# Attention in four chained layers: projection applied to the values, denominators inverted as four columns

## The reference

```python
qkv = einsum('bchw,oc->bohw', x, qkv_w)
qkv = depthwise_conv_3x3(qkv, dw_w)
q, k, v = split(qkv, 3); q, k = l2norm(q), l2norm(k)      # tokens are the 16384 pixels
attn = softmax(einsum('bnc,bmc->bnm', q, k) * temperature, axis=-1)
out = einsum('bnm,bmc->bnc', attn, v)
return einsum('bchw,oc->bohw', out, proj_w)               # 48x48
```

## Time and profile before

| | |
|---|---|
| median of 3 runs | 7465.26 us (7460.11 to 7467.92) |
| the profiled execution | 7462.4 us, its span 7460.1 us |
| attention stage, first score to last copy of the sums | 326.75 to 3114.90 us |
| TensorE busy in it | 2765.76 us |
| VectorE busy in it | 2643.70 us |
| ACT busy in it | 2368.25 us |

### The profile page before, as it was taken

The page is one execution under the profiler, slowest core; times in us unless marked ns, Lnnn a source line. Parts: engine busy times, 40 slices in busy tenths (PEclk is TensorE's granted clock), DMA queues, the critical chain, the costliest instruction groups (busy, mean ns, idle before and its releaser), DMA issues. The chain is left out here.

```text
span 7460.1 us, 169553 instructions
## 1 busy us (share of the span) xinstructions
PE 6090.7 (82%) x68803; PEld 2679.5 (36%) x69312; DVE 6843.6 (92%) x6229; ACT 5240.9 (70%) x5318; POOL 3429.0 (46%) x1801
## 2 busy tenths in 40 slices
PE   6899999999999999899767777777777777766330
PEld 3333333333333333366323333333333333333220
DVE  7799999999999999899789999999999999986776
ACT  3388888888888888633468888888888888842000
POOL 2000000000000000000169999999999999974777
PEclk9899999999999999999889999999999999987665
DMA  2200000000000000000110000000000000022333
GB/s 42 61 8 8 8 11 8 8 8 8 8 8 11 8 8 8 4 6 7 35 46 6 6 6 6 6 6 6 6 6 6 6 6 6 6 56 74 83 83 82
DMA packets 130880, 146.51 MB, mean 20 GB/s; under 512 B 52524, under 2 KB 111692, under 8 KB 129244
## 3 DMA queue, kind: packets, MB, share of 16 engines
q1 hardware_dynamic: 104160, 82.28, 4.0%
q0 software_dynamic: 24576, 50.36, 2.6%
q10 hardware_dynamic: 1440, 3.75, 0.3%
HBM read 98.55 MB, written 37.75 MB: 18 GB/s over the span
## 5 line engine op out<-in xcount | busy, mean ns | idle before, releaser
L1790 POOL TENSOR_TENSOR k_image<-k_image,s_b 128x1024 f32<-128x1024 f32 x1152 | 2700.8, 2355 | 118.1 <-ACT k_image L1703 83.5
L710 ACT ACTIVATE att_prob<-att_scores,a_bound,a_temp 128x1024 f32<-128x1024 f32 x2048 | 2357.0, 1202 | 420.8 <-PE att_scores L653 420.8
L721 DVE TENSOR_TENSOR att_prob_lo<-att_prob 128x1024 f16<-128x1024 f32 x2048 | 2429.0, 1238 | 139.4 <-ACT att_prob L710 123.0
L638 POOL TENSOR_TENSOR k_image<-k_image,att_rden 48x512 f32 x32 | 67.7, 2116 | 2990.4 <-DVE att_rden L733 2990.4
L1703 ACT COPY k_image<-h_du 128x1024 f32<-128x1024 f32 x1152 | 1166.4, 1013 | 322.9 <-PE h_du L1637 322.3
L1753 DVE TENSOR_TENSOR_SCAN h_state_odd<-h_keep,k_image 128x1024 f32<-128x1024 f32 x576 | 1378.4, 2509 | 0.0
L653 PE MATMUL att_scores<-att_queries,att_keys 32*128 32x512 f16 (+1 forms) x20480 | 1294.0, 377 | 21.5 <-DMA att_queries<-qk_halves 18.8
L1709 ACT ACTIVATE h_keep<-h_keep,h_decay 128x1024 f32<-128x1024 f32 x1152 | 1256.7, 1091 | 74.7 <-PE h_keep L1626 51.2
L670 PE MATMUL att_sums<-att_prob,a_values 128*64 128x512 bf16 x8192 | 1124.9, 395 | 0.0
L1626 PE MATMUL h_keep<-h_rows,h_spread 128*128 128x512 bf16 x2303 | 699.0, 385 | 510.6 <-DVE h_state_odd L1753 263.1
L653 PEld LDWEIGHTS att_scores<-att_queries,att_keys 32*128 32x128 f16 (+1 forms) x20480 | 439.7, 93 | 776.2 <-ACT att_prob L710 379.3
(11 more groups left out here) (295 smaller groups left out, 7021.1 us busy)
## 6 DMA issues: line engine op xcount, KB each, us to landing
y_rows<-h_y_sb SPq DMA_DIRECT2D x1024, 3.0 KB
att_queries<-qk_halves SPq DMA_DIRECT2D x124, 128.0 KB, 2.2
parts<-t_part SPq DMA_DIRECT2D x48, 192.0 KB, 2.5
h_rows<-parts SPq DMA_DIRECT2D x128, 72.0 KB
b_shared<-cells,b_index POOLq DMA_INDIRECT x512, 2.6
qk_halves<-qkv_hi SPq DMA_DIRECT2D x128, 48.0 KB, 1.6
cells<-b_shared SPq DMA_DIRECT2D x4, 1536.0 KB, 5.1
att_keys<-qk_halves SPq DMA_DIRECT2D x32, 128.0 KB, 2.7
```

The source lines that it names most:

```text
L710: nc.scalar.activation(prob[:, u % RING, :], scores[:, u % SLOTS_S, :], ACT.Exp, bias=bound[:, 0:1], scale=temp[:, 0:1]).then_inc(prob_rea ...
L721: nc.vector.tensor_tensor(prob_lo[:, u % RING, :], prob[:, u % RING, :], prob_hi[:, u % RING, :], ALU.subtract).then_inc(low_ready, 1)
L1790: nc.gpsimd.tensor_tensor(drive[k % 3], du_sb[k % 3], b[:, c * CH:(c + 1) * CH], ALU.mult).then_inc(drive_ready, 1)
```

## The change

The sum over keys and the projection are both linear, so the projection is moved from the sums to the values. In `turn`, the 8 transposes become 8 f32 matmuls that turn v and multiply it by `out_w`, now 48x48 (twice, for the two partition ranges). To keep the f16 halves of `values` in range, the first stage divides `out_w` by a bound of each output channel and keeps the bound in `out_scale`: one more absolute value on ACT, two small matmuls on TensorE, five operations on VectorE, in place of two copies there.

In the attention stage the projection matmul goes. ACT's copy at unit 6 now takes 113 rows. At unit 12 VectorE adds the two partial sums (`total`). SP stores the two denominator rows in DRAM (`den_rows`), loads them as 128 partitions x 2 x 4, VectorE adds and inverts them at unit 18 (`join_den`, `invert`: 128x4), SP stores that in DRAM and loads it back as 48 equal rows of 512, and from unit 28 VectorE makes 8 products of 48x64, three units apart (`divide`). SP's loop over blocks is unrolled; its query loads now have these five DMAs between them.

```diff
-PROJECT_AT = 12
-INVERT_FROM = 18
+TOTAL_AT = 12
+INVERT_AT = 18
+DIVIDE_FROM = 28
 ...
@@ load_and_prepare: tensor, vector
+            pe.wait_ge(out_absolute, 1)
+            nc.tensor.matmul(ps_o[:, 0:C], all_ones[:, :], out_abs[:, :], ...)
+            nc.tensor.matmul(ps_o[HI, C:C + 1], out_abs[:, :], all_ones[:, 0:1], ...)
-            for rows_in, one in ((slice(32, 64), V_ONE), (slice(96, P), 64 + V_ONE)):
-                then(nc.vector.tensor_copy(out_w[rows_in, LO], ident[rows_in, one:one + 1].broadcast_to([32, C])))
             count_quarter(3)
+            dve.wait_ge(out_summed, 2)
+            then(ts(out_inv[:, 0, :], ps_o[:, 0:C], 0.25, 1e-30, ALU.mult, ALU.max))
+            then(nc.vector.reciprocal(out_inv[:, 1, :], out_inv[:, 0, :]))
+            for part in (LO, HI):
+                then(tt(out_w[part, :], out_w[part, :], out_inv[part, 1, :], ALU.mult))
+            then(ts(out_scale[HI, :], ps_o[HI, C:C + 1], 0.25, 1e-30, ALU.mult, ALU.max))
@@ project_qkv: turn
-                        last = nc.tensor.transpose(turned[:, b, t, :], v_sb[part, t * P:(t + 1) * P], ident[part, part])
+                        last = nc.tensor.matmul(turned[:, b, t, :], v_sb[part, t * P:(t + 1) * P], out_w[part, :], start=True,
+                                                stop=True)
@@ attend: sync
+            def spread_den(b):
+                sp.wait_ge(sums_copied, b + 1)
+                for side in range(2):
+                    row = side * CHUNK + V_ONE
+                    sp.dma_start(den_rows[b, side:side + 1], sums_sb[row:row + 1, :]).then_inc(den_stored, 16)
+                sp.wait_ge(den_stored, 32 * (b + 1))
+                wait_past(sp, joined, b)
+                sp.dma_start(den[:, :, :], den_rows[b].rearrange("s (p k) -> p s k", p=P)).then_inc(den_loaded, 16)
+
+            def spread_inverse(b):
+                sp.wait_ge(inverted, b + 1)
+                sp.dma_start(inverse_rows[b].rearrange("(p k) -> p k", p=P), inverse[:, :]).then_inc(inverse_stored, 16)
+                sp.wait_ge(inverse_stored, 16 * (b + 1))
+                wait_past(sp, added, b)
+                sp.dma_start(rden[HI, :], inverse_rows[b].partition_broadcast(C)).then_inc(inverse_loaded, 16)
+            for n in range(2, NQB):
+                sp.wait_ge(scores_ready, (n - 1) * UNITS)
+                load_queries(n, n % 2)
+                spread_den(n - 2)
+                spread_inverse(n - 2)
@@ attend: tensor
-            def project(b):
-                pe.wait_ge(sums_copied, b + 1)
-                nc.tensor.matmul(sums[0:SPAN, b % 2, :], out_w[:, :], sums_sb[:, :], start=True, stop=True).then_inc(projected, 1)
@@ attend: scalar, copy_sums
-                nc.scalar.copy(sums_sb[:, :], sums[:, b % 2, :]).then_inc(sums_copied, 1)
+                wait_past(act, den_stored, 32 * b)
+                nc.scalar.copy(sums_sb[0:SPAN + 1, :], sums[0:SPAN + 1, b % 2, :]).then_inc(sums_copied, 1)
@@ attend: vector
-                nc.vector.reciprocal(rden[HI, q], sums[LO, b % 2, q]).then_inc(inverted, 1)
-                nc.vector.tensor_tensor(rden[HI, q], sums[HI, b % 2, q], rden[HI, q], ALU.mult).then_inc(divided, 1)
+            def total(b):
+                dve.wait_ge(sums_copied, b + 1)
+                nc.vector.tensor_tensor(sums_sb[HI, :], sums[HI, b % 2, :], sums_sb[LO, :], ALU.add).then_inc(totalled, 1)
+            def join_den(b):
+                dve.wait_ge(den_loaded, 16 * (b + 1))
+                nc.vector.tensor_tensor(inverse[:, :], den[:, 0, :], den[:, 1, :], ALU.add).then_inc(joined, 1)
+            def invert(b):
+                nc.vector.reciprocal(inverse[:, :], inverse[:, :]).then_inc(inverted, 1)
+            def divide(b, piece):
+                dve.wait_ge(totalled, b + 1)
+                dve.wait_ge(inverse_loaded, 16 * (b + 1))
+                nc.vector.scalar_tensor_tensor(out=rden[HI, q], in0=sums_sb[HI, q], scalar=out_scale[HI, 0:1],
+                                               in1=rden[HI, q], op0=ALU.mult, op1=ALU.mult).then_inc(divided, 1)
```

More of the change, by code:

```diff
@@ L230, in attention_layer, with load_and_prepare @@
             least = fn.sb("least", [SPAN, 1])
-            load_and_prepare(nc, image, ident, d, x_split, qk_split, v_split, ones, least, stats, out_w, bound, temp)
+            load_and_prepare(nc, image, ident, d, x_split, qk_split, v_split, ones, least, stats, out_w, out_scale,
+                             bound, temp)
             group_norm(nc, "gn0", image, gmean, norm, sems, False, stats_ready=stats)
-            project_qkv(nc, image, norm, ident, halves, values, x_split, qk_split, v_split, ones, least)
-        attend(nc, image, halves, values, out_w, bound, temp, stats)
-def load_and_prepare(nc, image, ident, d, x_split, qk_split, v_split, ones, least, stats, out_w, bound, temp):
+            project_qkv(nc, image, norm, out_w, halves, values, x_split, qk_split, v_split, ones, least)
+        attend(nc, image, halves, values, out_scale, bound, temp, stats)
+def load_and_prepare(nc, image, ident, d, x_split, qk_split, v_split, ones, least, stats, out_w, out_scale, bound, temp):
     with ExitStack() as ctx:
@@ L312, in _ @@
                                  start=True, stop=True).then_inc(v_sum, 1)
+            pe.wait_ge(out_absolute, 1)
+            nc.tensor.matmul(ps_o[:, 0:C], all_ones[:, :], out_abs[:, :], start=True, stop=True).then_inc(out_summed, 1)
+            nc.tensor.matmul(ps_o[HI, C:C + 1], out_abs[:, :], all_ones[:, 0:1], start=True, stop=True).then_inc(out_summed, 1)
         @block.scalar
@@ L324, in _ @@
                     nc.scalar.copy(split[half][HI, :, cols], split[half][LO, :, cols]).then_inc(copied, 1)
+            act.wait_ge(out_scaled, 2)
+            nc.scalar.activation(out_abs[:, :], out_w[LO, :], ACT.Abs).then_inc(out_absolute, 1)
             act.wait_ge(zeroed, 1)
             act.wait_ge(copied, 6)
+            act.wait_ge(out_absolute, 1)
         @block.vector
@@ L402, in conv3x3_pair, with project_qkv @@
     ins.then_inc(signal, 1)
-def project_qkv(nc, image, norm, ident, halves, values, x_split, qk_split, v_split, ones, least):
+def project_qkv(nc, image, norm, out_w, halves, values, x_split, qk_split, v_split, ones, least):
     with ExitStack() as ctx:
@@ L578, in _, with attend @@
             root(nblk - 1)
-def attend(nc, image, halves, values, out_w, bound, temp, stats):
+def attend(nc, image, halves, values, out_scale, bound, temp, stats):
     with ExitStack() as ctx:
@@ L626, in _ @@
             load_queries(1, 1)
[L627 to L630, removed]
+            for n in range(2, NQB):
[3 more added lines that the diff above has]
+                spread_inverse(n - 2)
+            for b in range(NQB - 2, NQB):
+                spread_den(b)
+                spread_inverse(b)
+            sp.wait_ge(den_loaded, 16 * NQB)
+            sp.wait_ge(inverse_loaded, 16 * NQB)
         @block.gpsimd
@@ L664, in weigh_high @@
                 if g == 0:
[L665 removed]
+                    wait_past(pe, totalled, b - 1)
                 pe.wait_ge(prob_ready, u + 1)
@@ L743, in _ @@
                     count(b - 1)
[L744 to L749, removed]
+                if b and g == TOTAL_AT:
+                    total(b - 1)
+                if b and g == INVERT_AT:
+                    join_den(b - 1)
+                    invert(b - 1)
+                piece, rest = divmod(g - DIVIDE_FROM, 3)
+                if b and rest == 0 and 0 <= piece < PIECES:
+                    divide(b - 1, piece)
+            total(NQB - 1)
+            join_den(NQB - 1)
+            invert(NQB - 1)
             for piece in range(PIECES):
-                invert(NQB - 1, piece)
                 divide(NQB - 1, piece)
```

37 lines of the change are left out of this document (20 added, 17 removed).

## The result

The changed kernel takes 7412.7 us (median of 4, 7410.06 to 7414.86) against 7465.92 for the kernel before: ratio 0.9927, 95% interval 0.9916 to 0.9939, 53.2 us less. The forecast was 7405, 60 less.

A forecast was written before the change was run, and what follows sets the result against it. TensorE's queue was taken to bound attention; -32.2 (projection), -30.7 (VectorE's lag) and +3.0 (tail) sum to -59.9, giving 7405 us. The range, to hold 8 in 10, was 7391 to 7431; the forecast's own terms, 7394 to 7416.

The forecast's parts named there:

- The pace: Attention: TensorE sets the block's time; each us put into its queue is a us of the block.
- Rival C: Attention: the loop over scores and exponentials sets the pace, gaps fill, only the tail stays; 7468 us, chance 0.03.
- The projection, -32.2: Attention: removing the projection matmul from TensorE's queue saves 1.04 us in each of 31 blocks, 32.2 us.
- VectorE's lag, -30.7: Attention: TensorE's two waits for a lagging VectorE, 0.99 us a block, go in 31 blocks, 30.7 us.
- The lead: Attention: VectorE can fall some 2.6 us behind, a lead of 6 units, before TensorE waits.
- rival A: Attention: only the projection's gain comes, as VectorE still lags past 2.6 us; 7436 us, chance 0.08.
- Waits added, 0: Attention: both DMA round trips, for denominators and inverse, are covered more than twice, so they cost 0.
- Rival D: Attention: the joining at unit 18 waits for its DMAs, price (wait - 2.6) x 31; 7480 us or more, chance 0.04.
- The convolution stage, 0: Convolution stage: f32 matmuls replacing transposes add 0.4 us, just inside TensorE's wait for VectorE; cost 0, up to 12 us.
- Rival B: Convolution stage: f32 matmuls take four times the transposes' length and lengthen it by 12 us; 7417 us, chance 0.11.
- First stage, 0: First stage: VectorE's added operations end 1.6 us before GpSimd's last clearing; cost 0, at worst 1 us.
- The tail, +3.0: After the last attention block: uncovered stores, loads, joining and products take 10.9 us instead of 7.9, +3.0.

The follow-up runs named there:

- e2: The kernel before, with VectorE's 8 reciprocals and 8 products a block replaced by 8 copies, projection kept: 7593.74 us, ratio 0.9952.
- e3: The changed kernel with 8 unused reciprocals of 48x64 a block put back on VectorE: 7621.99 us, ratio 0.9989.
- e4: The changed kernel with 4 unused reciprocals of 48x64 a block put back on VectorE: 7412.43 us, ratio 0.9933.
- e9: The changed kernel with 31 more f32 matmuls of 48 columns in TensorE's first stage, product overwritten: 7402.66 us, ratio 0.9923.
- e6: The changed kernel with total and joining at unit 7 and products from unit 8, every third unit: 7571.4 us, ratio 1.0145.
- rep_before: The kernel before, unchanged, run once more for its profile: 7627.65 us.

## Why the prediction was right

**The pace.** The step was that TensorE's queue sets it and nothing put into it is won back. It is shown both ways: the block lost what was taken out of the queue, and the matmul put back costs its full 0.86 us a block. Rival C is out.

**The projection, -32.2, and VectorE's lag, -30.7.** Both mechanisms and both sizes hold: `e2` alone gives 0.99 a block for the second and keeps the 1.04 of the first. The lead, taken as 2.6 us, is 2.74; it shrinks by the 0.32 a piece that was reckoned; and in the changed kernel it never falls under 1.5 before the end of the last block, so VectorE's lag is at most 1.2, where at most 1.9 was reckoned. So rival A had no ground. Together they gave 86.92 - 85.03 = 1.89 a block, 58.6 us, not 62.9. The missing 0.13 is spread over 32 distances: undisturbed they were 2.653 and are 2.657. In the mean over some 900 of them the extra 4 ns come at the first low-half matmuls. What makes them is open. It is not VectorE's work (2.653 in `e2`, as in the kernel before, and 2.657 to 2.658 in `e3` and `e4`), not the width of `out_w`'s tile, and not the queue's length (2.657 in `e9`).

**Waits added, 0.** Right, with the cover that was reckoned: loads landed in 1.7 and 2.7 us. Rival D's price was too low. `e6` tests it at the product, not at the joining: the wait beyond the lead is paid in full, and the lower clock after it comes on top, 1.46 us in the block shown.

**The convolution stage, 0.** Right in the end, and by luck in the margin. One pass more was reckoned as +0.4, and it is +0.64, more than TensorE's wait of 0.36. It stayed hidden because TensorE's lead lasted to the end of the stage. Rival B's factor of four came out as 2.7 (0.38 to 1.02 us).

**First stage, 0.** Right: GpSimd still ends it, and VectorE's five operations end 2 us before. That the first attention score came 1.8 us earlier is spread: the kernel before has it at 326.75 and, in `rep_before`, at 324.19.

**The tail, +3.0.** The part reckoned came to +1.9. The store and load of the denominators took 3.2 us instead of 4.2, those of the inverse 4.6 instead of 3.8, and the joining and the products 0.8 less than reckoned. Beside it the last units end sooner, because VectorE is no longer behind: last scoring to copy 5.5 us instead of 6.6, and 6.6 again in `e3`. Together +0.8.

**What no step had.** The standstill at the scan's end, +4.8. With it the sum is -58.6 + 0.8 + 4.8 = -53.0, and 53.2 less was measured. That it fits to 0.2 is partly luck: the runs of one kernel spread over 5 us and more, and the two profiled executions differ by 49.5 (in the changed kernel's the last layer took 4.5 us more and the first score came 1.8 earlier). The forecast's 60 was 7 too much, of which the standstill is 4.8 and the 4 ns a distance 4; the tail gave 2 back. The lower end of the forecast's own range, 7394, does not follow from its terms, which give about 7400.

The changed kernel's forecasts for its profile (no distance over 2.70 behind the first block, window about 2725, tail near 11) came out at 2.67 at most, 2728.5 and 9.8.

## What to carry to other kernels

Before costing a change in a pipeline, find the distance between two equal steps of the engine suspected as the bound, and list where it is longer: each excess is a term, and whether later steps come closer together afterwards tells if it is on the path. Work on an engine with slack cost nothing here until its lag exceeded the lead of 2.7 us, and in full beyond: reckon lag and lead in us, step by step. The DMA round trips were free with their waits 10 and 12 units (13.0 and 16.6 us) behind what they wait for. With the first product one unit behind its reciprocal they cost some 5 us a block, of which the wait was 3.0 and the clock at which TensorE came back 1.46 in the block shown.

## What the runs showed of the hardware

- A wait of 2.72 us in a stretch at full clock was followed by 4.6 us at a granted 0.63, which cost 1.46 us more; waits of 2.45 to 3.89 us were followed by the lower clock in 31 of 31 blocks, waits of 0.5 us in the kernel before in none.
- An f32 matmul of 512 columns costs TensorE 1.04 us with weights of 128x112 and 0.86 with 112x48; which of the two dimensions makes the difference is not separated.
- 8 f32 transposes of 48x128 take 0.38 us to the next start, 8 f32 matmuls of the same shape 1.02.
- A standstill of 4.6 us of TensorE went with 124 records more in its queue, 6.5 ms before it, and stayed with 512 more. One 16 KB packet of code starts per 256 TensorE records, and the standstill is where one comes after 468 to 492.
- One chip takes 164 us more than another in the layer that gathers by GpSimd's indirect DMAs, and 0.01 us more in each of attention's blocks.
